# Reversing the order of the stages inside each step of a software pipeline across TensorE and ScalarE

## The reference

```
x = layernorm(x + segment_sum(x[src] * edge_weight, dst))
x = layernorm(x + graph_attention(x, edges, attr5))          # two heads, softmax over each source's edges
x = layernorm(x + transformer_block(x, edges, attr32))       # q, k, v, softmax over each target's edges, Wp, MLP with Gelu
x = layernorm(x + elu(batchnorm(spline_conv(x, edges, attr3) + x @ root)))
```

```
out = agg.reshape(n, HC) @ Wp + bp
o = gelu(o @ W1 + b1) @ W2 + b2
```

## Time and profile before

| | us |
|---|---|
| Median of 3 runs | 10322.87 (10318.38 to 10327.56) |
| The profiled execution | 10327.56 |
| Its span, first to last instruction | 10325.4 |
| TensorE busy in it | 4415.4 (43%) |
| VectorE busy | 6367.2 (62%) |
| ScalarE busy | 4571.2 (44%) |
| GpSimd busy | 6537.0 (63%) |

### The profile page before, as it was taken

The page is one execution under the profiler, slowest core; times in us unless marked ns, Lnnn a source line. Parts: engine busy times, 40 slices in busy tenths (PEclk is TensorE's granted clock), DMA queues, the critical chain, the costliest instruction groups (busy, mean ns, idle before and its releaser), DMA issues. The chain is left out here.

```text
span 10325.4 us, 101390 instructions
## 1 busy us (share of the span) xinstructions
PE 4415.4 (43%) x24136; PEld 3359.7 (33%) x24136; DVE 6367.2 (62%) x7868; ACT 4571.2 (44%) x6523; POOL 6537.0 (63%) x6626
## 2 busy tenths in 40 slices
PE   1112678782000000000003366666665577877776
PEld 1111577771000000000003344445444344444444
DVE  7888777774221321219996588888887555555554
ACT  1111577771211211116773377777775233333332
POOL 6767777775677777770002677777775277777774
PEclk9999877775555555555555677777776799999997
DMA  3333322222332332325552444444443377777773
GB/s 102 100 93 103 78 79 75 70 88 28 117 115 100 119 115 101 115 88 202 205 205 78 100 140 136 134 139 139 136 133 100 115 236 235 237 237 237 237 237 108
DMA packets 722783, 1395.94 MB, mean 135 GB/s; under 512 B 409551, under 2 KB 439452, under 8 KB 715094
## 3 DMA queue, kind: packets, MB, share of 16 engines
q0 software_dynamic: 287072, 587.19, 20.3%
q1 hardware_dynamic: 406786, 639.32, 18.6%
q10 hardware_dynamic: 28852, 168.65, 4.5%
HBM read 827.48 MB, written 602.51 MB: 138 GB/s over the span
## 5 line engine op out<-in xcount | busy, mean ns | idle before, releaser
L822 POOL DMA_INDIRECT l_rows<-in_x,l_idx x1568 | 1635.9, 1043 | 689.1 <-issue 448.7
L2450 POOL DMA_INDIRECT l_rows<-table,l_idx x1568 | 1483.2, 946 | 663.4 <-issue 462.3
L1925 POOL DMA_INDIRECT l_rows<-h,l_idx x1568 | 1526.5, 974 | 574.7 <-issue 445.0
L1303 POOL DMA_INDIRECT rows<-l_rows,l_idx x1568 | 1501.2, 957 | 525.1 <-issue 497.2
L1960 PE MATMUL l_made<-l_kv_w,l_rows_t 128*128 128x256 f32 x3136 | 1081.8, 501 | 773.6 <-ACT l_kv L1990 452.5
L1698 PE MATMUL l_wide<-l_diag,l_ones 128*128 128x384 f32 x4 | 3.3, 928 | 3126.5 <-DVEq L1728 3126.5
L2471 PE MATMUL l_half<-l_rows,identity 128*128 128x512 f32 x1568 | 906.1, 662 | 426.6 <-DMA l_rows<-table,l_idx 423.5
L1960 PEld LDWEIGHTS l_made<-l_kv_w,l_rows_t 128*128 128x128 f32 x3136 | 754.2, 258 | 976.5 <-issue 848.2
L2569 ACT ACTIVATE l_diag<-identity,l_up 128x128 f32<-128x128 f32 x1568 | 500.7, 390 | 1208.6 <-PE l_half L2473 1184.6
L1698 PEld LDWEIGHTS l_wide<-l_diag,l_ones 128*128 128x128 f32 x4 | 1.0, 312 | 3127.4 <-DVEq L1728 3127.4
L1259 ACT COPY l_rows<-l_run 128x1792 f32<-128x1792 f32 x56 | 191.6, 3421 | 1559.9 <-POOLq L88 1519.2
(11 more groups left out here) (396 smaller groups left out, 13207.4 us busy)
## 6 DMA issues: line engine op xcount, KB each, us to landing
sums<-l1s_out ACTq DMA_DIRECT2D x56, 1988.0 KB, 6.9
sums<-l_out SPq DMA_DIRECT2D x112, 924.0 KB, 4.2
spread<-zeros SPq DMA_DIRECT2D x28, 3612.0 KB, 12.8
l_spread<-spread SPq DMA_DIRECT2D x112, 903.0 KB
l1s_rows<-rows SPq DMA_DIRECT2D x56, 1008.0 KB, 5.4
spread<-zeros SPq DMA_DIRECT2D x56, 938.0 KB
l_spread<-spread SPq DMA_DIRECT2D x56, 938.0 KB, 4.5
sums<-l_out ACTq DMA_DIRECT2D x56, 896.0 KB, 3.7
```

Source lines behind the costliest of these rows:

```text
L822: pool.indirect_dma_start(rows[:, b, t], None, a["x"], bass.IndirectOffsetOnAxis(ap=idx[:, b, t:t + 1], axis=0)) \
L1303: pool.indirect_dma_start(g["rows1_d"], bass.IndirectOffsetOnAxis(ap=idx[:, b, t:t + 1], axis=0), rows[:, b, t], None).then_inc(sent[b], 16)
L1925: pool.indirect_dma_start(rows[:, c.r, t, 0:C], None, g["h2_d"], bass.IndirectOffsetOnAxis(ap=idx[:, c.r, t:t + 1], axis=0)).then_inc(got[ ...
L2450: pool.indirect_dma_start(rows[:, b, t], None, g["table3_d"], bass.IndirectOffsetOnAxis(ap=idx[:, b, t:t + 1], axis=0)) \
```

## The change

Inside a step, TensorE and ScalarE take the stages in descending order, so the oldest group comes first and the newest last. For TensorE and two stages the sequence becomes T0, M0, T1, M1 in place of T0, T1, M0, T2, M1. The waits and their counts are the same, and so are all instructions.

```
     def tensor(self, pe, work):
 
         for step in range(len(self.groups) + self.stages - 1):
-            for k in range(self.stages):
+            for k in reversed(range(self.stages)):
                 i = step - k
                 if not 0 <= i < len(self.groups):
                     continue
...
     def scalar(self, act, work):
         last = self.stages - 1
         for step in range(len(self.groups) + last - 1):
-            for k in range(last):
+            for k in reversed(range(last)):
                 i = step - k
                 if not 0 <= i < len(self.groups):
                     continue
```

## The result

The changed kernel took 10386.23 us in the median of 6 runs (10377.53 to 10390.74), the kernel before 10318.87 (10316.41 to 10327.56): a ratio of 1.0062, 95% interval 1.005 to 1.0075, slower by 52 to 77 us. Forecast were 10382 us and +59.

A forecast was written before the change was run, and what follows sets the result against it. TensorE was taken to bound l1n and l2c, busy nearly throughout, and l2m. Terms of 40.0 + 14.9 + 0 + 0 + 4 gave +59 us on the median of 10322.87, so 10382 us, range 10350 to 10402.

The forecast's parts named there:

- The hole: Two-stage pipelines: T(i+1) (transposes) queues behind M(i) (matmuls), which waits for ScalarE's copy of group i, now uncovered.
- The rival that TensorE reads on past the wait: Two-stage pipelines: T(i+1) starts anyway while M(i) waits, so the time stays 10323 us; chance 0.03.
- The clock stays at 1.2 GHz in all of l1n and l2c: Both projections run wholly at granted clock 0.50, as root does now with smaller holes: +40.0 and +14.9 us.
- l1n: Layer 1's node projection, 25 groups of two tiles: 82.4 us against 42.4, +40.0.
- l2c: The attention block's projection, 13 groups of four tiles: 41.8 us against 26.9, +14.9.
- Both clock rivals: l1n and l2c: clock rises after some 22 us (+32, chance 0.13), or at once (+14 to +19, 0.06).
- The size of a step: Two-stage chain of transposes, copy, matmuls: 3.35 us at 1.2 GHz, 2.21 us at 2.4 GHz.
- L2m +4: Three-stage MLP pipeline: steps of 2.7 to 2.9 us against 2.47 (+2.7), plus 1.6 behind C(2): together +4.
- the 1.6 of B and A: L2m: one B (two 512-column passes) and one A (four transposes) now follow C(2), last matmuls awaiting VectorE: 1.6 us.
- L2a 0: Layer 2's query projection: hidden by GpSimd's 49 scatters; the store of `table2` has 21.8 us of room; cost 0.
- Root 0: Layer 3's pipeline: steps 2.98 to 3.35 us, block 4.4 us later, within 5.6 us of room before `more`; cost 0.
- The sum: All five blocks: 40.0 + 14.9 + 0 + 0 + 4 = 59 us, giving 10382; chance 0.70.

The follow-up runs named there:

- the pair of runs with spare matmuls: 16 spare matmuls ahead of l1n and of l2c: with the new order ratio 1.0075, with the old order 1.001, both against the kernel before.
- the fillers: New order plus a spare matmul behind each group's transposes in l1n and l2c: 256 columns, ratio 1.0042 against before; 512 columns, 10337.53 us in one execution.
- l2m alone: Kernel before with the new order only in the three-stage MLP pipeline, on TensorE and ScalarE: ratio 0.9993, block 42.5 us.
- after, again: The changed kernel measured once more beside the kernel before on the same chip: 10386.73 against 10315.16 us, ratio 1.0071.
- l2a and root alone: Kernel before with the new order only in layer 2's query projection and layer 3's pipeline: ratio 1.0002.
- the run with l2m's TensorE order: Kernel before with only TensorE's order reversed in the three-stage MLP pipeline, ScalarE's as before: ratio 1.0031, block 70.4 us.

## Why the prediction was right, point by point

- *The hole.* Right. M waits for its copy in every step, and T(i+1) doesn't start meanwhile. The rival that TensorE reads on past the wait is out.
- *The clock stays at 1.2 GHz in all of l1n and l2c.* Right, argued from root's rows; shown by the windows of after. Both clock rivals are out, and the pair of runs with spare matmuls, and the fillers, show it as a cost of its own. The choice of root as the nearest row carried the forecast: l2a, with holes too, had 1.00. That the clock rises after about 22 us without a hole was read from one execution; in others it was 7, 14 and 19.
- *The size of a step.* 3.35 us was read where the transposes met an empty TensorE (1.17 from loads to copy). Behind M's matmuls it is 1.31 (5633.77 to 5635.08), and the step 1.31 + 0.58 + 0.05 + 1.56 = 3.50. So l1n is +44.1, not +40.0, and l2c +17.2, not +14.9.
- *L2m +4.* +2.8, and +3.7 in the profiles of l2m alone and of after, again. The step of 2.88 lies in the forecast's 2.7 to 2.9. But ten steps of 0.41 and the 1.6 of B and A are 5.7. The sum came out near by luck: behind C(2) before had a stretch at 0.50 that after doesn't have, and its steps of 3.43 and 4.65 us instead of 2.47 made before 3.1 us longer. The windows view of before, then of after:

```profile
8104.60:8111.00 6.40, 6.40 (x17) 2.88 (x16) 0.47 (x2) 1.84 (x3) 0.00 (x0) 0.50 0.00 0
```

```profile
8137.00:8164.00 27.00, 23.77 (x126) 13.72 (x125) 4.18 (x11) 10.41 (x19) 0.00 (x0) 1.00 0.00 1
```

- *L2a 0.* Right. Its clock was high, the store slipped by 9.9 us where 8 were forecast, and the room was 21.8.
- *Root 0.* Right in the sum here, wrong in the margin. The step is 3.76, not 3.35: ScalarE waits for T(i+1) before it writes the result of group i, so that result (0.27 until the copy starts) now lies in the chain as well. The block became 8.7 us longer, not 4.4 (10225.91 to 10272.24 against 10188.68 to 10226.27), and of the 10.0 us between `more`'s last load and the first of L1099's last additions in the earlier trace rows 0.13 were left (1.37 in the profile of l2a and root alone). The forecast had 5.6. The last load's own result was needed 1.8 us after that first addition, so a chain longer by more than some 1.8 us would have shown, and on the chip where TensorE stalls in root there was no room at all.
- *The sum.* 59 against 64 in the three blocks and +67 and +72 in the two pairs of medians. The 64 lies in both intervals; whether the new order also makes the attention loop's long form more frequent is left open. The sum is 5 low in the blocks, since the low-clock step was put 0.15 us too short.

## What to carry to other kernels

In a two-stage pipeline on one in-order engine the newest group must be issued before the oldest is waited for: with the order reversed, double buffers are there and nothing overlaps. The price of such a hole on TensorE is first the hole, and then possibly the clock; here they were 39 and 22 of 61 us, and a block at the low clock that is given the high one back gains 42. The nearest stalled block of the same kernel, root, read in the windows view, told which clock to expect; l2a would have told the opposite, so such a reading can fail. When a stage off the changed path scatters by more than the effect, compare block times between fixed instructions, and use totals only for what is larger.

## What was not expected of the hardware

- Work that is thrown away can pay: a spare 512-column matmul in each step shortened l1n from 86.2 to 57.3 us and l2c from 43.7 to 30.3, by raising the granted clock from 0.50 to 1.00. A 256-column one raised it in l1n only, though TensorE counted as busy in 43.71 of 44.00 us of l2c.
- The same l1n in the old order was at 0.50 for its first 7 us in one profile (35.1 us in the run with l2m's TensorE order) and for 22 in another (42.1 in before). L2c was 19.6 and 26.5 us in the same two.
- Holes didn't decide the clock alone: in after, l2a with holes had 1.00 where l1n and l2c with holes had 0.50.
- The attention loop has two paces, 115 to 119 and 122 to 127 us of TensorE in 200 us, between executions and within one; nothing run here shows why.
